# Maxima matmuls of two heads side by side on the two halves of the array, with a second copy of the odd heads' q and k

## The chip, the cores and the metric

One core of one Trainium2 chip runs the whole kernel. The metric is the device time of that core in microseconds (us), the median of three runs. The engines are TensorE (PE for its matmuls, PEld for its weight loads in the profile), VectorE (DVE), ScalarE (ACT), GpSimd (POOL) and SyncE (SP), which here only issues DMAs.

## The reference

A post-norm transformer block on x of 8 batches x 256 tokens x 128 features, in two layers.

```
q, k, v = x @ Wq.T + bq, x @ Wk.T + bk, x @ Wv.T + bv     # 16 heads of 64
q, k    = rope(q), rope(k)
attn    = softmax(q @ k.T / 8) @ v                        # per batch and head, 256 x 256
x       = layernorm(x + attn @ Wo.T + bo)
gates   = softmax(x @ gate_w); the best 2 of 8 experts, both weighted by the sum of their gates
x       = layernorm(x + sum over chosen experts of gelu(x @ w1[e] + b1[e]) @ w2[e] + b2[e], weighted)
```

The softmax needs the maximum of each row of q @ k.T, and how these row maxima come about is what the change is about.

## The kernel before, in words

**Units and slots.** The attention is cut into 16 units (`UNITS`) of 8 heads (`UH`); two units make a batch. Every engine runs the same hand-written order of slots T = -3 to 16, and slots 1 to 12 are three rounds of a hardware loop. In slot T the unit T is attended (scores, exp, times v), the row maxima of unit T + 1 are finished and those of unit T + 2 begun, and unit T + 3 is projected and rotated. Each slot has eight places i = 0 to 7. `maxima_at` gives the head whose maxima are found at place i: heads 3 to 7 of unit T + 1 at places 0 to 4, heads 0 to 2 of unit T + 2 at places 5 to 7. TensorE and VectorE walk these places in the same order, each in its own queue.

**Maxima.** For each head, `maxima` (line 348) issues two matmuls of 64 rows x 128 columns of weights and 256 moving columns: q of 128 tokens against k of all 256, contraction over the 64 features on partitions 0 to 63 of `qk`. Their results fill one PSUM bank, `ps_s[h % 2]`. VectorE's `row_maxima` (line 808) reduces the bank to two maxima per partition and raises `max_done`. The wait in `maxima` asks for the reduction of head h - 2, the last reader of that bank. At h == 0 `maxima` also waits for `qk_in`, that is, until all DMAs that bring unit u into `qk` have landed.

**From maxima to scores.** After head 7, `turn_maxima` (line 358) transposes the 16 columns of maxima, `read_mT` (line 815) copies them out, and a DMA of SP (line 299) writes them into row 64 of the q part of `qk`, whose k part holds ones there. So the matmuls of `scores` (line 365), which contract over all 128 partitions, subtract the maximum by themselves. ACT's exp reads `ps_t` (line 656), and `times_v` (line 375) multiplies by v in four matmuls of 65 columns per head.

**From projection to qk.** `project` (line 334) makes q and k of unit T + 3, ACT adds the bias (`raw`, line 638), VectorE multiplies by cosine and sine (line 785) and combines them in `rope` (lines 805 and 806), once for each half of the heads. The second `rope` stands at place 6, behind `find_maxima(5)`, which is the first head of unit T + 2, `read_mT`, `invert_sums`, `times_sin` and `find_maxima(6)`, and in every second slot behind `ln_one` step 1 (line 852) as well. When `rope_ready` has come, SP issues 8 DMAs of 64 KB (line 309) that gather the heads from `roped` into `qk`, one after another. The gate of unit u + 1 is then the wait at its head 0, at place 5 of the next slot.

**The rest.** In even slots from 2 on (`close`), the batch just finished is transposed (`turn_o`, line 395), multiplied by Wo (`out_proj`, line 405) and normalised by VectorE in ten small steps (`ln_one`, lines 852 to 892), most of them at places 6 and 7. `value` (line 345) makes v of a later unit at place 6 and waits for `ln_one` step 1 in those slots. The experts follow after slot 16 and are not touched.

Of the kernel before, what the change touches and what calls it, by code (L numbers as in the profile page):

```python
# [8 lines left out]
BF16 = mybir.dt.bfloat16  # L9
# [4 lines left out]
P = 128  # L14
S = 256
HID = 128
NH = 16
DH = 64
NB = 8
TOK = NB * S  # L20
UH = 8
# [9 lines left out]
EPS = 1e-5  # L31
EARLY = 3
M_ROW = 64
ROPE_DMAS = 8
TWO_ONES = 0x3F803F80


# [19 lines left out]
def postln_block(nc, x, packed_b, packed_f, expert_of, out):  # L57
# [15 lines left out]
    with ExitStack() as ctx:  # L73
        def sb(name, shape, dt):
            return ctx.enter_context(nc.sbuf_tensor(name, shape, dt))

        def sem(name):
            return ctx.enter_context(nc.semaphore(name))
# [29 lines left out]
        by_sin = sb("by_sin", [P, 2, 2, 2, S], BF16)  # L108
        roped = sb("roped", [P, 2, 2, 2, 2, S], BF16)
        qk = sb("qk", [P, 4, 2, UH, S], BF16)  # L110
        v_sb = sb("v_sb", [P, 2, 2, NH, DH + 1], BF16)
        row_max = sb("row_max", [P, 2, UH, QT], BF16)
        mT_sb = sb("mT_sb", [UH * QT, 2, P], BF16)
# [59 lines left out]
        def bank(name):  # L173
            return ctx.enter_context(nc.psum_tensor(name, [P, 512], F32))

        ps_s = [bank(f"ps_s{i}") for i in range(2)]
# [23 lines left out]
        qk_in = [sem(f"qk_in{i}") for i in range(4)]  # L200
# [3 lines left out]
        s_ready = sem("s_ready")  # L204
        max_done = sem("max_done")
# [50 lines left out]
        def need(eng, s, value):  # L256

            if isinstance(value, int) and value <= 0:
                return
            eng.wait_ge(s, value)  # L260

        def run(eng, slot):

            for T in range(-3, 1):
                slot(T, 0)
            with eng.Fori(0, 3) as it:
                for T in range(1, 5):
                    slot(T, it)
            for T in range(13, 17):
                slot(T, 0)  # L270

        def n(it, per_unit, units, more=0):

            return it * (4 * per_unit) + (per_unit * units + more)

        def has(T):

            return dict(attend=0 <= T < UNITS, maxima=0 <= T + 1 < UNITS, value=0 <= T + 2 < UNITS,
                        project=0 <= T + 3 < UNITS, close=T in range(2, UNITS, 2))


        @block.sync
        def _(sp):
            first, end = PACK_B["wqk0"][0], PACK_B["xT0"][1]
            sp.dma_start(in_b[:, first:end], packed_b[:, first:end]).then_inc(in_first, 16)
            sp.dma_start(in_b[:, 0:first], packed_b[:, 0:first]).then_inc(in_second, 16)
            sp.dma_start(in_b[:, end:COLS_B], packed_b[:, end:COLS_B]).then_inc(in_rest, 16)
            sp.dma_start(x_sb[:], x).then_inc(in_rest, 16)

            def slot(T, it):  # L290
                s = has(T)
                if s["maxima"]:
                    u = T + 1

                    need(sp, mT_ready, n(it, 1, u, 1))
                    if T == -1:
                        sp.wait_ge(pad_ready, 4)
                    dst = qk[M_ROW:M_ROW + 1, u % 4, 0, :, :]
                    sp.dma_start(dst, mT_sb[:, u % 2, :]).then_inc(m_in[u % 2], 16)
                if s["project"]:  # L300
                    u = T + 3

                    need(sp, rope_ready, n(it, 2, u, 2))
                    for g in range(4):
                        for half in range(2):
                            from_g = roped[32 * g:32 * g + 32, u % 2, half].rearrange("p a j s -> p (a j) s")
                            to = qk[32 * half:32 * half + 32, u % 4, :, :, :].rearrange(
                                "p a (j g) s -> p (a j) g s", g=4)[:, :, g, :]
                            sp.dma_start(to, from_g).then_inc(qk_in[u % 4], 16)
                if T == -3:  # L310
                    sp.dma_start(in_f[:], packed_f).then_inc(in_late, 16)
                    sp.dma_start(exp_of[:], expert_of).then_inc(in_late, 16)

            run(sp, slot)
            for p, (first, count) in enumerate(PIECES):
                sp.wait_ge(y_out, p + 1)
                sp.dma_start(out[:, first:first + count, :], y_sb[:, p % 2, 0:count]).then_inc(stored[p % 2], 16)
            for i in range(2):
                sp.wait_ge(stored[i], 16 * len(PIECES[i::2]))
# [3 lines left out]
        def _(pe):  # L323
# [22 lines left out]
                                 start=True, stop=True).then_inc(v_proj, 1)  # L346

            def maxima(u, h, it):
                if h == 0:
                    need(pe, qk_in[u % 4], it * (16 * ROPE_DMAS) + 16 * ROPE_DMAS * (u // 4 + 1))  # L350
                need(pe, max_done, n(it, UH, u, h - 1))
                for t in range(QT):
                    mm = nc.tensor.matmul(ps_s[h % 2][:, t * S:t * S + S],  # L353
                                          qk[0:DH, u % 4, 0, h, t * P:t * P + P],
                                          qk[0:DH, u % 4, 1, h, :], start=True, stop=True)
                mm.then_inc(s_ready, 1)

            def turn_maxima(u, it):
                take(1, mT_ready, n(it, 1, u, 1))
# [132 lines left out]
            def slot(T, it):  # L492
# [3 lines left out]
                def find_scores(i):  # L496
                    for u, h in maxima_at(T, i):
                        maxima(u, h, it)
# [269 lines left out]
        def _(dve):  # L768
# [27 lines left out]
            def rope(u, g, it):  # L796
# [3 lines left out]
                if g == 0:  # L800

                    w = 16 * ROPE_DMAS * ((u - 2) // 4 + 1)
                    need(dve, qk_in[(u - 2) % 4], it * (16 * ROPE_DMAS) + w)
                r, c, s = roped[:, u % 2, :, :, g, :], by_cos[:, g], by_sin[:, g]
# [433 lines left out]
```

## Time and profile before

| What | Value |
|---|---|
| Time, median of 3 runs | 293.36 us (292.1 to 294.01) |
| Profiled execution: its own time, its span | 295.25 us, 293.5 us |
| PE busy | 246.1 us (84%) |
| DVE busy | 235.9 us (80%) |
| ACT busy | 168.0 us (57%) |
| Mean granted clock of TensorE | 0.819 |

Busy times are those of the profiled execution. Ends of matmuls are modelled, so the starts of matmuls are the firmer marks. The granted clock is a share of 2.4 GHz; 0.50 is 1.2 GHz.

### The profile page before, as it was taken

The page shows a single profiled execution, that of the slowest core. Times are in us where ns is not written, and L with a number is a line of the kernel's source. Part 1 is how long each engine was busy: PE and PEld are TensorE (multiplying, and loading weights), DVE is VectorE, ACT ScalarE, POOL GpSimd, SP SyncE. Part 2 cuts the span into 40 slices and gives each one's busy share as a digit, 9 for nine tenths or more (in the row PEclk, how much of TensorE's full clock was granted, in tenths as well). Part 3 has the DMA queues.
Part 4 walks back from the last instruction along what each step waited for, and adds up shares of the span by engine and source line. Part 5 has one row for each costly group of instructions (what it writes and reads, how often), then busy time and mean ns, then how long its engine had stood idle before and what let it go on. Part 6 is the DMA issues. An engine that isn't in the chain of part 4 may idle for free.

```text
span 293.5 us, 5981 instructions
## 1 busy us (share of the span) xinstructions
PE 246.1 (84%) x1785; PEld 139.2 (47%) x1785; DVE 235.9 (80%) x688; ACT 168.0 (57%) x327; POOL 20.6 (7%) x34
## 2 busy tenths in 40 slices
PE   2737999997789789979988797999799938899991
PEld 0111345464446444645555355546545725466671
DVE  5898786969996989699798969897985794656985
ACT  3901556676858575846677574858534645545210
POOL 5000000000000000000000000000080010000121
PEclk9999999999955965685597859558855797999997
DMA  7153113030302021111113030303120000000012
GB/s 276 59 135 72 37 36 75 1 74 2 74 22 54 22 53 29 43 36 36 45 27 72 1 72 1 72 1 72 27 47 1 0 4 0 2 0 2 36 40 71
DMA packets 20438, 12.66 MB, mean 43 GB/s; under 512 B 2732, under 2 KB 19396, under 8 KB 20420
## 3 DMA queue, kind: packets, MB, share of 16 engines
q1 hardware_dynamic: 20420, 12.44, 16.5%
q8 instruction: 9, 0.15, 0.2%
q14 instruction: 9, 0.07, 0.1%
HBM read 2.92 MB, written 1.05 MB: 14 GB/s over the span
## 4 chain that ended last, share of the span: by engine, by line
issue 71%; PE 17%; DVE 7%; ACT 2%; POOL 2%; POOLq 0%; DVEq 0%
PE ps_o L487 4%; PE ps_s L461 3%; PE ps_t L370 2%; PE ps_s L353 2%; POOL sd L742 1%; PE ps_t L471 1%; PE ps_o L385 1%; PE ps_o L485 1%; ACT hg L715 1%; PE ps_m L448 1%; DVE qk L778 1%; DVE qk L777 1%; ACT oT_sb L651 1%; POOL rs L764 1%; PE ps_m L395 1%
## 5 line engine op out<-in xcount | busy, mean ns | idle before, releaser
L812 DVE TENSOR_REDUCE row_max<-ps_s 128x2 bf16<-128x512 f32 x128 | 86.7, 679 | 20.9 <-PE ps_s L353 19.7
L656 ACT ACTIVATE probs<-ps_t 128x512 bf16<-128x512 f32 x128 | 74.6, 606 | 35.4 <-PE ps_t L370 35.0
L353 PE MATMUL ps_s<-qk 64*128 64x256 bf16 x256 | 67.5, 359 | 7.5 <-DMA qk<-roped 4.8
L370 PE MATMUL ps_t<-qk 128*128 128x256 bf16 x256 | 66.5, 355 | 3.5 <-DMA qk<-mT_sb 1.7
L638 ACT ACTIVATE raw<-ps_m,bqk 128x256 bf16<-128x256 f32 x128 | 51.2, 478 | 9.3 <-PE ps_m L338 5.4
L385 PE MATMUL ps_o<-v_sb,probs 128*128 128x65 bf16 x512 | 46.5, 224 | 3.7 <-DVE o_sb L834 3.2
L385 PEld LDWEIGHTS ps_o<-v_sb,probs 128*128 128x128 bf16 x512 | 41.0, 121 | 16.2 <-issue 5.9
L645 ACT CAST v_sb<-ps_m 128x512 bf16<-128x512 f32 x32 | 17.5, 590 | 47.1 <-PE ps_m L345 47.1
L338 PE MATMUL ps_m<-in_b 128*128 (+1 forms) x128 | 35.3, 396 | 7.8 <-DMA in_b<-in_packed_b 4.6
L370 PEld LDWEIGHTS ps_t<-qk 128*128 128x128 bf16 x256 | 16.5, 106 | 42.3 <-issue 26.1
L834 DVE TENSOR_TENSOR o_sb<-ps_o,r_sum 128x256 bf16<-128x256 f32 x64 | 26.4, 412 | 0.1
L353 PEld LDWEIGHTS ps_s<-qk 64*128 64x128 bf16 x256 | 15.8, 103 | 22.5 <-DVE row_max L812 6.8
L338 PEld LDWEIGHTS ps_m<-in_b 128*128 128x128 bf16 x128 | 15.9, 135 | 19.0 <-ACT raw L638 7.8
L345 PE MATMUL ps_m<-in_b 128*128 128x512 bf16 x32 | 14.4, 525 | 12.3 <-DVE attn L852 9.1
L785 DVE TENSOR_TENSOR by_cos<-raw,in_b 128x1024 bf16<-128x1024 bf16 x32 | 21.9, 684 | 1.7 <-ACT raw L638 1.6
L742 POOL TENSOR_TENSOR sd<-ve,half_b 128x2 bf16<-128x2 bf16 x8 | 5.6, 705 | 239.9 <-DVE ve L879 239.9
L785 DVE TENSOR_TENSOR by_sin<-raw,in_b 128x1024 bf16<-128x1024 bf16 x32 | 21.4, 669 | 0.0
L715 ACT ACTIVATE hg<-ps_s,in_f 128x512 f32<-128x512 f32 x16 | 11.1, 691 | 17.1 <-PE ps_s L461 17.1
L825 DVE RECIPROCAL r_sum<-ps_o 128x4 f32<-128x4 f32 x64 | 11.1, 173 | 11.3 <-PE ps_o L385 10.7
L1104 DVE TENSOR_TENSOR hs<-hg,ps_t 128x512 f32<-128x512 f32 x16 | 11.0, 685 | 8.5 <-ACT hg L715 7.0
L651 ACT COPY oT_sb<-ps_m 128x1024 bf16<-128x1024 bf16 x16 | 15.7, 1036 | 1.0 <-PE ps_m L395 1.0
L487 PE MATMUL ps_o<-in_f,hs 128*128 128x128 f32 x112 | 16.2, 288 | 0.0
(105 smaller groups left out, 222.7 us busy)
## 6 DMA issues: line engine op xcount, KB each, us to landing
qk<-roped SPq DMA_DIRECT2D x128, 64.0 KB, 2.1
out<-y_sb SPq DMA_DIRECT2D x3, 256.0 KB, 2.1
in_b<-in_packed_b SPq DMA_DIRECT2D x1, 706.0 KB, 5.9
in_f<-in_packed_f SPq DMA_DIRECT2D x1, 586.0 KB
in_b<-in_packed_b SPq DMA_DIRECT2D x1, 516.0 KB, 3.8
in_b<-in_packed_b SPq DMA_DIRECT2D x1, 512.0 KB, 4.7
x_sb<-in_x SPq DMA_DIRECT2D x1, 512.0 KB, 6.7
qk<-mT_sb SPq DMA_DIRECT2D x16, 4.0 KB, 1.7
```

The costliest lines, as they stand in the source:

```text
L338: mm = nc.tensor.matmul(ps_m[a][:, half * S:half * S + S], wqk[u % 2][:, a, 2 * g + half, :], xT_sb[:, bass.ds(tok, S)], start=True, stop= ...
L353: mm = nc.tensor.matmul(ps_s[h % 2][:, t * S:t * S + S], qk[0:DH, u % 4, 0, h, t * P:t * P + P], qk[0:DH, u % 4, 1, h, :], start=True, sto ...
L370: mm = nc.tensor.matmul(ps_t[h % 2][:, c * S:c * S + S], qk[:, u % 4, 1, h, c * P:c * P + P], qk[:, u % 4, 0, h, :], start=True, stop=True)
L385: mm = nc.tensor.matmul(ps_o[(h // 2) % 2][:, col:col + DH + 1], probs[:, h % 4, c, t * P:t * P + P], v_sb[:, (u // 2) % 2, c, head, :], s ...
L487: mm = nc.tensor.matmul(y, hs[:, tc % 2, c, t * P:t * P + P], w2_sb[:, c, :], start=False, stop=(c == NE - 1))
L638: last = nc.scalar.activation(raw[:, u % 2, g, a, half, :], ps_m[a][:, half * S:half * S + S], ACT.Identity, bias=bqk[:, a, chunk:chunk + 1])
L645: nc.scalar.copy(v_sb[:, (u // 2) % 2, u % 2, UH * c:UH * c + UH, 0:DH], ps_m[c][:].rearrange("p (h d) -> p h d", d=DH)).then_inc(v_ready, 1)
L651: nc.scalar.copy(oT_sb[:, t].rearrange("p c s -> p (c s)"), ps_m[t][:].bitcast(BF16)).then_inc(oT_ready, 1)
L656: nc.scalar.activation(probs[:, h % 4].rearrange("p c s -> p (c s)"), ps_t[h % 2][:], ACT.Exp, scale=DH ** -0.5).then_inc(exp_done, 1)
L785: nc.vector.tensor_tensor(by[:, g].rearrange("p a h s -> p (a h) s"), raw[:, u % 2, g].rearrange("p a h s -> p (a h) s"), table[:].unsquee ...
L812: nc.vector.tensor_reduce(row_max[:, u % 2, h, :], ps_s[h % 2][:].rearrange("p (t s) -> p t s", s=S), AX_X, ALU.max, negate=True).then_inc ...
L834: nc.vector.tensor_tensor(o_sb[:, b % 2, :, head:head + 2, :].rearrange("p t h d -> p h t d"), o[:, :, 0:DH].rearrange("p (h t) d -> p h t ...
```

## The change

SP issues four more DMAs per unit: the odd groups of heads also go from `roped` to a new tensor `qk_odd`, on partitions 64 to 127, double buffered by unit. They raise the same semaphore as the eight others, so the gate of a unit now asks for twelve. `maxima` does nothing for an odd head. For an even head h it waits for the reductions up to head h - 1, and then issues the four matmuls of heads h and h + 1 in turn: even head from partitions 0 to 63 into `ps_s[0]`, odd head from partitions 64 to 127 into `ps_s[1]`. VectorE's work and order stay as they are.

```diff
-ROPE_DMAS = 8
+ROPE_DMAS = 12
...
+        qk_odd = sb("qk_odd", [P, 2, 2, UH // 2, S], BF16)
...
+                    for i in range(2):
+                        g = 2 * i + 1
+                        for half in range(2):
+                            from_g = roped[32 * g:32 * g + 32, u % 2, half].rearrange("p a j s -> p (a j) s")
+                            to = qk_odd[DH + 32 * half:DH + 32 * half + 32, u % 2, :, :, :].rearrange(
+                                "p a (j i) s -> p (a j) i s", i=2)[:, :, i, :]
+                            sp.dma_start(to, from_g).then_inc(qk_in[u % 4], 16)
...
             def maxima(u, h, it):
+
+                if h % 2 == 1:
+                    return
                 if h == 0:
                     need(pe, qk_in[u % 4], it * (16 * ROPE_DMAS) + 16 * ROPE_DMAS * (u // 4 + 1))
-                need(pe, max_done, n(it, UH, u, h - 1))
+                need(pe, max_done, n(it, UH, u, h))
                 for t in range(QT):
-                    mm = nc.tensor.matmul(ps_s[h % 2][:, t * S:t * S + S],
-                                          qk[0:DH, u % 4, 0, h, t * P:t * P + P],
-                                          qk[0:DH, u % 4, 1, h, :], start=True, stop=True)
-                mm.then_inc(s_ready, 1)
+                    even = nc.tensor.matmul(ps_s[0][:, t * S:t * S + S],
+                                            qk[0:DH, u % 4, 0, h, t * P:t * P + P],
+                                            qk[0:DH, u % 4, 1, h, :], start=True, stop=True)
+                    odd = nc.tensor.matmul(ps_s[1][:, t * S:t * S + S],
+                                           qk_odd[DH:P, u % 2, 0, h // 2, t * P:t * P + P],
+                                           qk_odd[DH:P, u % 2, 1, h // 2, :], start=True, stop=True)
+                even.then_inc(s_ready, 1)
+                odd.then_inc(s_ready, 1)
```

## Rows read from the trace of the kernel before

**Rows 1.** Page, part 1: busy time, share of the span, instructions.

```profile
PE 246.1 (84%) x1785; PEld 139.2 (47%) x1785; DVE 235.9 (80%) x688; ACT 168.0 (57%) x327; POOL 20.6 (7%) x34
```

**Rows 2.** Windows, TensorE alone: length, busy (count), granted clock, DMA share, GB/s.

```profile
40.00:43.00 3.00, 3.00 (x16) 1.00 0.00 0
...
85.00:88.00 3.00, 3.00 (x20) 0.50 0.22 50
...
100.00:103.00 3.00, 2.76 (x29) 1.00 0.29 66
```

**Rows 3.** Windows, one two-slot round: PE, PEld, DVE, ACT, POOL busy, clock, DMA.

```profile
109.17:123.45 14.28, 14.28 (x94) 8.09 (x92) 11.10 (x27) 10.10 (x20) 0.00 (x0) 0.54 0.16 37
123.45:137.62 14.17, 12.29 (x94) 7.06 (x91) 12.74 (x40) 8.81 (x20) 0.70 (x1) 0.70 0.16 37
```

**Rows 4.** Timeline at 1.2 GHz: start, length, engine, line, count, idle before.

```profile
107.87 0.60 PE L353 MATMUL ps_s<-qk 64*128 64x256 bf16 x2
108.41 0.13 PEld L370 LDWEIGHTS ps_t<-qk 128*128 128x128 bf16 x2 [0.41 <-issue]
...
108.81 0.43 PE L385 MATMUL ps_o<-v_sb,probs 128*128 128x65 bf16 x4
...
109.12 0.66 DVE L812 TENSOR_REDUCE row_max<-ps_s 128x2 bf16<-128x512 f32 x1
109.17 0.60 PE L353 MATMUL ps_s<-qk 64*128 64x256 bf16 x2
```

**Rows 5.** Timeline, TensorE, two and four matmuls of a projection at 1.2 GHz.

```profile
86.45 0.63 PE L338 MATMUL ps_m<-in_b 128*128 x2
...
88.18 1.06 PE L338 MATMUL ps_m<-in_b 128*128 x4
```

**Rows 6.** Timeline at 2.4 GHz, gate of unit 8 and the scores behind it.

```profile
123.45 0.39 PE L353 MATMUL ps_s<-qk 64*128 64x256 bf16 x2
...
123.77 0.39 PE L370 MATMUL ps_t<-qk 128*128 128x256 bf16 x2
```

**Rows 7.** Timeline at the start: DMAs of units 0 and 1, and their gates.

```profile
11.82 5.25 SPq L309 DMA_DIRECT2D qk<-roped  x8
...
18.56 0.61 PE L353 MATMUL ps_s<-qk 64*128 64x256 bf16 x2 [4.14 <-DMA qk<-roped]
...
21.09 5.10 SPq L309 DMA_DIRECT2D qk<-roped  x8
...
27.70 0.61 PE L353 MATMUL ps_s<-qk 64*128 64x256 bf16 x2 [0.63 <-DMA qk<-roped]
```

**Rows 8.** DMA issues by line: KB each, median us from issue to landing.

```profile
qk<-roped SPq DMA_DIRECT2D x128, 64.0 KB, 2.1
```

**Rows 9.** Timeline, from the gate of unit 7 (109.17) to unit 8's DMAs.

```profile
111.29 0.69 DVE L812 TENSOR_REDUCE row_max<-ps_s 128x2 bf16<-128x512 f32 x1
...
113.63 0.41 DVE L806 TENSOR_TENSOR roped<-by_cos,by_sin 128x512 bf16<-128x512 bf16 x1
...
114.06 5.13 SPq L309 DMA_DIRECT2D qk<-roped  x8
```

**Rows 10.** Timeline, from the gate of unit 8 to unit 9's DMAs, a closing slot.

```profile
127.32 0.40 DVE L852 TENSOR_TENSOR attn<-ps_m,v_bias 128x256 bf16<-128x256 f32 x1
...
128.41 1.89 SPq L309 DMA_DIRECT2D qk<-roped  x3
```

**Rows 11.** Timeline, TensorE, gates of unit 2 and of unit 15 (14 gates in all).

```profile
40.02 0.61 PE L353 MATMUL ps_s<-qk 64*128 64x256 bf16 x2
...
218.64 0.61 PE L353 MATMUL ps_s<-qk 64*128 64x256 bf16 x2
```

**Rows 12.** Timeline after a closing slot: maxima of head 4, reduction of head 3.

```profile
102.22 0.39 PE L353 MATMUL ps_s<-qk 64*128 64x256 bf16 x2
...
104.32 0.69 DVE L812 TENSOR_REDUCE row_max<-ps_s 128x2 bf16<-128x512 f32 x1 [0.26 <-issue]
```

**Rows 13.** Timeline at the start: the reductions of unit 0 and what they wait for.

```profile
21.78 0.28 DVE L898 CAST o_bias<-ps_m 128x128 bf16<-128x128 f32 x1
...
23.72 3.47 DVE L812 TENSOR_REDUCE row_max<-ps_s 128x2 bf16<-128x512 f32 x5 [1.07 <-PE ps_s L353]
24.47 1.20 PE L353 MATMUL ps_s<-qk 64*128 64x256 bf16 x4 [0.36 <-DVE row_max L812]
```

**Rows 14.** Waits of DVE from 40.02 to 218.64: total, times, longest.

```profile
DVE row_max L812 <- PE ps_s L353: 12.5, 22, 1.2
DVE r_sum L825 <- PE ps_o L385: 7.7, 10, 0.9
```

## The prediction

> **What bounds the kernel now.** I read the busy table first. TensorE is busy 84%, VectorE 80% [rows 1], too close for shares to decide, so the next view is windows of 3 us along the attention. The reader is to see two regimes. Where the granted clock is 0.50 TensorE is busy 3.00 of 3.00 us; where it is 1.00 it has gaps [rows 2]. The windows before the first clock record show 1.00, but the maxima matmuls there last 0.61 us for two as at 0.50, not 0.39 as at 1.00 [rows 6, 11], so I count that stretch as 1.2 GHz. At the low level TensorE is the bound. Over a two-slot round of 28.45 us VectorE is busy 23.84 us, 12.74 in one half and 11.10 in the other [rows 3]; it is the next bound, and it still spends 12.5 us on waits for maxima and 7.7 us on waits for times v between 40 and 218.6 us [rows 14]. The measure of progress is the gate, the first maxima matmul of each unit: from unit 2 at 40.02 to unit 15 at 218.64, 13 slots in 178.62 us, 13.74 us each or 27.5 us per two [rows 11].
>
> **Less work on TensorE.** At 1.2 GHz the two matmuls of one head occupy TensorE from 107.87 to 108.41, 0.54 us [rows 4]. Two of 256 columns stream in 0.43 us, the difference between four and two in a row [rows 5]; the other 0.11 us lies ahead of the next weight load, which sat idle for 0.41 us on "issue" behind the maxima [rows 4]. At 2.4 GHz a head costs 0.32 us [rows 6]. A pair costs between 0.54 us (the halves run fully side by side) and 0.97 us (one after the other, 4 x 0.213 + 0.11). I take 0.64, as one weight load of about 0.1 us must come before the second half starts. A dropped odd head also drops the way back into 64-row matmuls: four of 65 columns stream in 0.22 us at 1.2 GHz, and the next maxima start 0.36 us after them [rows 4], so that way costs 0 to 0.14; I take 0.1. A pair saves 2 x 0.54 - 0.64 + 0.1 = 0.54 us at 1.2 GHz, four pairs about 2.2 us per slot.
>
> By the Trainium skill, TensorE: Matmul & The Clock Gate, Part 3 (The mechanism), matmuls on different row groups run concurrently and start about 4 ns apart. By it the pair would cost 0.54 and not 0.64 us, and with the sum below, where a pair stands once in each return leg, the result would be about 1.4 us lower. No run shown yet has such a pair.
>
> **Four more DMAs on SP's queue, on the path.** Eight issues take 5.25 us at the start and 5.13 in the steady state, 0.65 us each [rows 7, 9], and a DMA lands 2.1 us after its issue [rows 8]. The gate opens at the last landing: unit 0's first issue is at 11.82 and its gate at 18.56; unit 1's are 21.09 and 27.70. So the way from first issue to open gate is 6.7 us with eight [rows 7], and with twelve 6.7 + 4 x 0.65 = 9.3 us. Bounds: 6.7, if the new copies were issued in no time, and 10.1, if each also added half a transfer time; I keep 9.3, the rate of the rows being the same in two stages.
>
> Is that hidden? Before, unit 7's gate is at 109.17, unit 8's DMAs start at 114.06 and its gate is at 123.45, 9.4 us later [rows 6, 9]: 2.7 us of slack with eight, 0.1 with twelve. In other slots the distance is smaller, so the DMAs become the gate. Then a loop closes over each slot. Gate of unit u; return leg to the first DMA of unit u + 1; 9.3 us to its gate. The return leg is what VectorE does from place 5 to the second rope. Before it is 4.89 us (109.17 to 114.06) in one slot and 4.96 us (123.45 to 128.41) in the closing one, but VectorE came to the head only at 111.29 [rows 6, 9, 10]. If it stands waiting at the gate, it starts 0.64 us after it, needs 111.29 to 114.06 = 2.77 us of work, and waits some 0.65 us for times v of head 3, which TensorE reaches behind the pair, scores and transpose: 4.1 us. In a closing slot step 1 of the normalisation adds 0.4 us [rows 10] and some 0.1 of wait, 4.6 us, up to 5.0 where the output projection runs at 1.2 GHz. Two slots: 4.1 + 4.6 + 2 x 9.3 = 27.3 us, up to 27.7. What is queued behind the gate on TensorE is everything: scores, transpose, times v and so exp and VectorE's next inputs. SP itself has room: its twelve issues end 7.8 us after the first, and the next mT DMA comes later than that.
>
> **The stricter wait.** Head h now waits for the reduction of h - 1. After a closing slot the maxima of head 4 were issued at 102.22 and the reduction of head 3, behind the LayerNorm steps, ended at 104.32 + 0.69 = 105.01 [rows 12]: 2.8 us late. At head 0 of unit 7 it would be 0.6 us (109.17 against 109.12 + 0.66) [rows 4]. VectorE is the late one there and loses only what TensorE needs to restart, about 0.64 us less the 0.4 us of other work that stands between, plus what times v comes later: 0.3 to 1.5 us per closing slot. VectorE's bound for two slots is then 23.84 plus waits; with 1.8 us of waits per slot as before (23 us of 13 slots with the small ones) [rows 14], 27.4 us. So chain and VectorE stand at the same length, and I take 27.5 us per two slots, no gain against 27.5. TensorE's 2.2 us per slot go into its waiting at the gate.
>
> **The start.** Unit 0's gate moves by 2.6 us to 21.2. VectorE then reduces head 0 and reads the biases, ending near 23.6 (before, 21.78 + 0.28) [rows 13], and head 1 by 24.3. Before, the reductions ran back to back at 0.69 us, with TensorE filling one bank while the other was read [rows 13]. Now each pair is 2 x 0.69 us of reductions and then about 0.75 us of restart: head 6 ends near 29.9, two products of 0.65 follow, head 7 ends at 31.9. Unit 1's DMAs would have landed at 21.09 + 9.3 = 30.4, but its pair waits for head 7: gate at 32.0 in place of 27.70. Unit 2's first DMA comes at about 36.0, and its gate at 45.3 in place of 40.02: +5.3 us. Slots 2 and 3, without LayerNorm, take 13.4 us each, as before.
>
> **The end.** From unit 15's gate on there are no rope DMAs. Four pairs at 1.2 GHz remain: -2.2 us. What follows is unchanged.
>
> **Sum.** Against the profiled execution's 295.25 us (span 293.5 and 1.75 around it): +5.3 at the start, 0 in 13 slots, -2.2 at the end, +3.1. I take half a microsecond off for the first slots' pairs at 1.2 GHz, where a little less TensorE work precedes each rope: +2.6. The median of the runs shown is 293.36, so 296 us, 0.9% slower. The profiled run lies 0.6% above the median; the difference is carried over, not the level.
>
> **Rivals.**
> - **TensorE's relief wins.** If copies land sooner than I add (6.7 to 8 us to the gate), the return leg no longer closes the loop and VectorE bounds: 23.84 us and about 2 of waits, 25.9 per two slots. From unit 4 on that is 5.5 x (27.6 - 25.9) = -9.4; with +4.3 at the start and -2.2 at the end, about 286 us. For it: TensorE was saturated at the low clock [rows 2]. Against: the serial issue on SP [rows 7, 9]. A middle case, waits of 1.4 us a slot, gives 291. The Trainium skill's TensorEngine Tiling (Array Packing), PSUM Bottleneck, says that tiling does not speed up the emptying of PSUM, which may then bound; VectorE's 23.84 of 28.45 us agrees, and it is this case's floor.
> - **The halves don't run side by side.** The pair costs 0.97, 0.33 more than I took, once in each return leg and 14 times: +4.6, and the tail saves 1.1 less: 302 us. For it: matmuls on TensorE start in the order of the queue, and no row before shows two at once.
> - **The stricter wait decides (the other side).** The place is head 4 behind a closing slot, the price 1.3 us of VectorE each, decisive as soon as VectorE comes to head 3 later than TensorE comes to head 4, which 102.22 against 105.01 shows. Six such slots give +7.8 us on top of the start: about 303 us if VectorE and not the DMA loop sets the round.
> - **The clock.** More waiting at gates may keep the clock at 0.50 for longer; the return legs of six closing slots rise by 0.4: +2.4, 298 us. It lies inside the forecast's range.
>
> **Chances and range.** Forecast 0.55 (291.5 to 300), TensorE's relief 0.2 (half of it at 286, half at 291), serial halves 0.1, stricter wait 0.15. A change of 1% is about what a measurement of this kernel can tell: 290.4 and 296.3 bound "same". From the forecast 0.02 faster, 0.27 same, 0.26 slower; relief gives 0.14 faster and 0.06 same; the other two are slower but for 0.03. So faster 0.16, same 0.36, slower 0.48. The range 288 to 303 leaves out half of the relief case and a little of the others.
>
> **What would show it.** In the profile after: twelve issues in about 7.8 us per unit; TensorE's idle time ahead of the maxima put down to the DMA of `roped`, about ten times; 9.3 us from first issue to gate; gates 13.7 us apart; unit 2's gate near 45; a pair that ends within 0.65 to 0.75 us. I am wrong if the gates wait for nothing, if the first two gates move by less than 2 us, or if the gaps at maxima are those behind VectorE's reductions.

## The result, and the profile after

The changed kernel takes 305.6 us (median of 4 runs, 304.14 to 307.35) against 293.69 us before (292.1 to 294.05); the ratio is 1.042, 95% interval 1.034 to 1.050. I had forecast 296 us with a range up to 303: the sign was right, the size three to five times too small. The profiled execution is the shortest run, 304.14 us with a span of 302.3, and that of the kernel before, 295.25 us with a span of 293.5, lies above its other four; so the traces show 8.8 us of the 11.9 us between the medians, and the rest is the scatter of the runs. Medians and ranges are of all runs; the ratios, here and below, leave out runs that lie more than 1.5% above the fastest of their kernel.

First the busy line of the page (busy time, share of the span, instructions), to be held against [rows 1].

```profile
PE 203.5 (67%) x1785; PEld 122.0 (40%) x1785; DVE 238.0 (79%) x688; ACT 166.4 (55%) x327; POOL 20.6 (7%) x34
```

TensorE lost 43 us of busy time and the kernel became longer, so in the changed kernel TensorE's work no longer sets the pace. Next the view of waits of the changed kernel (total, times, longest).

```profile
PE ps_s L364 <- DVE row_max L827: 34.0, 26, 3.2
...
PE ps_s L364 <- DMA qk_odd<-roped: 30.5, 10, 6.7
...
DVE row_max L827 <- PE ps_s L367: 27.0, 42, 2.0
```

Two new waits stand ahead of the maxima matmuls (line 364), of nearly the same size: one for the last copy into `qk_odd` (30.5 us), one for VectorE's reductions (34.0 us). VectorE in its turn waits 27.0 us for the maxima. These are two of the mechanisms of the prediction, at once; the first is the sign that it had named for the forecast, about ten waits for the DMA, the second one that it had named against it.

The timeline shows where each acts: the gates of units 8, 9 and 10 with the rope DMAs between them, answering [rows 4, 6, 9].

```profile
131.91 0.39 PE L364 MATMUL ps_s<-qk 64*128 64x256 bf16 x1 [2.61 <-DMA qk_odd<-roped]
131.91 0.39 PE L367 MATMUL ps_s<-qk_odd 64*128 64x256 bf16 x1
...
132.45 0.61 PE L385 MATMUL ps_t<-qk 128*128 128x256 bf16 x2
...
136.41 5.21 SPq L310 DMA_DIRECT2D qk<-roped  x8
141.66 2.53 SPq L317 DMA_DIRECT2D qk_odd<-roped  x4
...
147.20 0.28 PE L364 MATMUL ps_s<-qk 64*128 64x256 bf16 x1 [1.45 <-DVE row_max L827]
...
151.43 5.11 SPq L310 DMA_DIRECT2D qk<-roped  x8
156.58 2.53 SPq L317 DMA_DIRECT2D qk_odd<-roped  x4
...
160.56 0.28 PE L364 MATMUL ps_s<-qk 64*128 64x256 bf16 x1 [2.84 <-DMA qk_odd<-roped]
```

From 151.43 to 160.56 are 9.13 us from first issue to gate, near the forecast 9.3; the gate opens with the DMA. But between 136.41 and 147.20 are 10.8 us: there the last DMA had landed at 145.65, and the gate waited for the reduction of head 7. The reader is to see two kinds of slots, closing ones (with the LayerNorm) and plain ones. The windows say the same (columns as in [rows 3]).

```profile
131.91:147.20 15.29, 10.31 (x91) 6.48 (x92) 12.00 (x36) 8.45 (x18) 0.69 (x1) 0.79 0.23 52
147.20:160.56 13.36, 7.47 (x91) 4.93 (x91) 12.10 (x29) 10.15 (x20) 0.00 (x0) 1.00 0.26 59
```

The closing slot takes 15.29 us and is set by VectorE: 12.00 us of work, and 3.29 us in which it is idle, 2.7 of them waiting for TensorE (0.7 in the closing slot of [rows 3]). The plain one takes 13.36 us and is set by the DMA loop. Together 28.65 us, against the 27.5 that I had taken. Inside the closing slot the loss begins behind the LayerNorm. The timeline of the changed kernel there:

```profile
136.49 0.28 PE L364 MATMUL ps_s<-qk 64*128 64x256 bf16 x1
...
139.97 0.42 DVE L907 TENSOR_SCALAR x<-attn,rs 128x128 bf16 x2
140.31 0.68 DVE L827 TENSOR_REDUCE row_max<-ps_s 128x2 bf16<-128x512 f32 x1
...
141.05 0.28 PE L364 MATMUL ps_s<-qk 64*128 64x256 bf16 x1 [2.42 <-DVE row_max L827]
...
141.47 0.69 DVE L827 TENSOR_REDUCE row_max<-ps_s 128x2 bf16<-128x512 f32 x1 [0.15 <-PE ps_s L367]
...
142.62 0.18 DVE L840 RECIPROCAL r_sum<-ps_o 128x4 f32<-128x4 f32 x1 [0.46 <-PE ps_o L400]
...
144.58 0.69 DVE L827 TENSOR_REDUCE row_max<-ps_s 128x2 bf16<-128x512 f32 x1 [0.84 <-PE ps_s L367]
```

Heads 2 and 3 are issued at 136.49 and stand ready; head 3 is reduced at 140.31, after `ln_one`. TensorE stands still for 2.42 us until then, starts heads 4 and 5 at 141.05, and everything that it does from there on is late: VectorE waits 0.15 us for head 4, 0.46 us for times v, 0.84 us for head 6. The 2.42 us of TensorE would be nothing, VectorE being busy; the 1.45 us of VectorE are the price.

Over the whole, the gates of units 2 and 15, against [rows 11], and what the stretches between them took:

```profile
45.73 0.39 PE L364 MATMUL ps_s<-qk 64*128 64x256 bf16 x1 [3.51 <-DMA qk_odd<-roped]
...
231.03 0.28 PE L364 MATMUL ps_s<-qk 64*128 64x256 bf16 x1 [0.31 <-DMA qk_odd<-roped]
```

| Stretch | Before | After | Difference | Forecast |
|---|---|---|---|---|
| to the gate of unit 2 | 40.02 | 45.73 | +5.7 | +5.3 |
| 13 slots, to the gate of unit 15 | 178.62 | 185.30 | +6.7 | 0 (and -0.5 for the first slots) |
| to the end of the span | 74.9 | 71.3 | -3.6 | -2.2 |

The 6.7 us lie in the closing slots alone. The six of them (from the gates of units 4, 6, 8, 10, 12 and 14 to the next) took 82.1 us before and 91.3 us after, 9.3 more; the seven plain ones took 96.6 and 94.0 us, 2.6 less.

### The profile page after: what moved, and what is told of

Same layout as the page of the kernel before. It is cut to its first block, busy times and chain, and to the rows that moved or that the text cites. A ratio compares the mean times of both kernels' runs of the same rounds, so it can differ in the third digit from the quotient of the medians.

```text
span 302.3 us, 6036 instructions
## 1 busy us (share of the span) xinstructions
PE 203.5 (67%) x1785; PEld 122.0 (40%) x1785; DVE 238.0 (79%) x688; ACT 166.4 (55%) x327; POOL 20.6 (7%) x34
## 4 chain that ended last, share of the span: by engine, by line
issue 73%; PE 14%; DVE 7%; ACT 2%; POOL 2%; DMA 1%; POOLq 0%; DVEq 0%
PE ps_o L502 4%; PE ps_s L476 3%; POOL sd L757 1%; PE ps_t L486 1%; DVE row_max L827 1%; PE ps_t L385 1%; ACT oT_sb L666 1%; PE ps_o L500 1%; DMA qk<-mT_sb 1%; ACT hg L730 1%; PE ps_m L420 1%; PE ps_m L463 1%; DVE qk L793 1%; DVE qk L792 1%; POOL rs L779 1%
## 5 line engine op out<-in xcount | busy, mean ns | idle before, releaser
L827 DVE TENSOR_REDUCE row_max<-ps_s 128x2 bf16<-128x512 f32 x128 | 86.8, 681 | 27.9 <-PE ps_s L367 27.0
L364 PE MATMUL ps_s<-qk 64*128 64x256 bf16 x128 | 32.2, 344 | 64.6 <-DVE row_max L827 34.0
L385 PE MATMUL ps_t<-qk 128*128 128x256 bf16 x256 | 61.4, 332 | 4.6 <-ACT probs L671 3.2
L653 ACT ACTIVATE raw<-ps_m,bqk 128x256 bf16<-128x256 f32 x128 | 50.4, 479 | 3.8 <-DVE bqk L795 3.8
L400 PE MATMUL ps_o<-v_sb,probs 128*128 128x65 bf16 x512 | 43.6, 216 | 4.2 <-DVE o_sb L849 3.8
L400 PEld LDWEIGHTS ps_o<-v_sb,probs 128*128 128x128 bf16 x512 | 37.5, 114 | 16.4 <-issue 7.9
L346 PE MATMUL ps_m<-in_b 128*128 (+1 forms) x128 | 29.8, 345 | 12.6 <-ACT raw L653 7.2
L364 PEld LDWEIGHTS ps_s<-qk 64*128 64x128 bf16 x128 | 7.7, 101 | 74.3 <-DVE row_max L827 37.1
L367 PE MATMUL ps_s<-qk_odd 64*128 64x256 bf16 x128 | 32.3, 344 | 0.0
L385 PEld LDWEIGHTS ps_t<-qk 128*128 128x128 bf16 x256 | 17.7, 107 | 24.7 <-issue 17.5
L346 PEld LDWEIGHTS ps_m<-in_b 128*128 128x128 bf16 x128 | 11.9, 114 | 25.2 <-ACT raw L653 16.5
```

What stands on the lines that cost most here:

```text
L346: mm = nc.tensor.matmul(ps_m[a][:, half * S:half * S + S], wqk[u % 2][:, a, 2 * g + half, :], xT_sb[:, bass.ds(tok, S)], start=True, stop= ...
L364: even = nc.tensor.matmul(ps_s[0][:, t * S:t * S + S], qk[0:DH, u % 4, 0, h, t * P:t * P + P], qk[0:DH, u % 4, 1, h, :], start=True, stop= ...
L367: odd = nc.tensor.matmul(ps_s[1][:, t * S:t * S + S], qk_odd[DH:P, u % 2, 0, h // 2, t * P:t * P + P], qk_odd[DH:P, u % 2, 1, h // 2, :], ...
L385: mm = nc.tensor.matmul(ps_t[h % 2][:, c * S:c * S + S], qk[:, u % 4, 1, h, c * P:c * P + P], qk[:, u % 4, 0, h, :], start=True, stop=True)
L400: mm = nc.tensor.matmul(ps_o[(h // 2) % 2][:, col:col + DH + 1], probs[:, h % 4, c, t * P:t * P + P], v_sb[:, (u // 2) % 2, c, head, :], s ...
L653: last = nc.scalar.activation(raw[:, u % 2, g, a, half, :], ps_m[a][:, half * S:half * S + S], ACT.Identity, bias=bqk[:, a, chunk:chunk + 1])
```

## The experiments

All ratios are to the kernel before, run beside each.

**Copies and gate alone.** `maxima` as before, with the change's twelve DMAs and its gate of twelve.

> The four extra DMAs per unit and the gate of twelve, but the maxima matmuls and their wait as before. Theory 1 (each slot is set by its own longest: the DMA gate in plain slots, the reductions in closing slots; the two add): the way from first issue to gate is 9.3 us, unit 2's gate moves by about 5 us, and the slots that took 12.3 to 13.1 us take 13.5 to 14, so 300 to 304 us. Theory 2 (the copies alone make the whole loss): 304 to 307 us. Theory 3 (only the stricter wait costs): within 2 us of before.

Measured: 303.74 us, ratio 1.040 (1.034 to 1.045). Its view of waits has the DMA ahead of the maxima twelve times:

```profile
PE ps_s L361 <- DMA qk_odd<-roped: 26.8, 12, 6.7
```

So the copies on the path cost 4% where nothing is paired. The time lies at the upper end of theory 1 and just below theory 2; it speaks against theory 3.

**The stricter wait alone.** The kernel before with one line changed:

```diff
-                need(pe, max_done, n(it, UH, u, h - 1))
+                need(pe, max_done, n(it, UH, u, h - h % 2))
```

> The kernel before with one edit: an even head waits for the reduction of the head just before it, the odd head waits as before. No copies, no pairs. Theory 1: TensorE stalls at heads 0, 4 and 6 behind VectorE, 1 us or more per slot, so 298 to 304 us. Theory 2: within 2 us of before. Theory 3: 304 to 307 us.

Measured: 310.8 us, ratio 1.058 (1.047 to 1.069). All three theories are off: the wait alone costs more than the whole change, and theory 1's 298 to 304 was too low. Both costs are real, and each alone, on a TensorE without the pairs' relief, loses as much as the whole change (4.2%) or more. Their sum, 9.8%, is more than twice the change's 4.2%, so the pairs give back a good part, or the costs cover each other. The next experiments remove them one at a time from the changed kernel.

**Fine gates.** The same twelve DMAs in another order on three semaphores; heads 0, 1, 4, 5 need the first four, 2, 3, 6, 7 the next, `scores` the last.

```diff
+                    for g, odd, done in ((0, 0, qk_in), (1, 1, qk_in), (2, 0, qk_in2), (3, 1, qk_in2),
+                                         (1, 0, qk_in3), (3, 0, qk_in3)):
...
+                if h == 2:
+                    need(pe, qk_in2[u % 4], it * 64 + 64 * (u // 4 + 1))
```

> The changed kernel with its twelve DMAs in another order and on three semaphores: heads 0, 1, 4 and 5 wait for four DMAs (about 4.1 us from the first issue), heads 2, 3, 6 and 7 for the next four, the scores for the last four. Theory 1: no gate waits for a DMA any more except at the start, the closing slots stay at 15.3 us and the plain ones fall to 12 to 13, so 295 to 300 us, 5 to 10 below the changed kernel. Theory 2: back at 293 or below. Theory 3: no change from 305.6.

Measured: 290.29 us, ratio 0.992 (0.988 to 0.997). The gate of twelve cost 5 points of ratio. It was the gate and its order, not the traffic: all twelve DMAs are still issued on the same queue. The number is the one that theory 2 gave, 293 or below, and under theory 1's 295 to 300; but the slots are theory 1's. The plain ones fell, to 11.6 to 12.2 us and so further than its 12 to 13, and the closing ones stayed long, as it has it (gates 30.3, 41.9, 54.0, 65.6, then 80.9 and 92.5: steps of 11.6, 12.1, 11.6, then 15.3 and 11.6).

**Reductions of a pair together.** At the place of the even head VectorE reduces both.

```diff
                     for u, h in maxima_at(T, i):
-                        row_maxima(u, h, it)
+                        if h % 2 == 0:
+                            row_maxima(u, h, it)
+                            row_maxima(u, h + 1, it)
```

> The changed kernel, but VectorE reduces both heads of a pair at the place of the even head, so that the banks are free one place earlier. Twelve DMAs and gate as in the change. Theory 1: closing slots fall from 15.3 to the DMA loop's 13.6 to 14, plain slots stay at 13.4, so about 296 to 300 us. Theory 2: no change from 305.6. Theory 3: back at 293 or below.

Measured: 299.97 us, ratio 1.027 (1.021 to 1.034), as theory 1 has it. The DMA now stands ahead of the maxima 15 times with 41.6 us, and at every gate but that of unit 1, so the loop took over the closing slots too.

**Both.**

> The gates of the fine-gates kernel and the reductions of a pair at one place together. Theory 1 (the DMA gate and the stricter wait are the two costs, and they add because each slot is set by its own longest): with both gone VectorE's work is the bound, 23.8 us and some 2 of waits per two slots, so 280 to 286 us. A rival: the pairs' own gain is small and what is left is VectorE and the clock, so no better than the fine gates alone, 288 to 291 us.

Measured: 291.86 us, ratio 0.994 (0.990 to 0.998). Here theory 1 failed, and the time came out just above the rival's 288 to 291. The waits of TensorE for reductions fell from the 42.1 us of the fine-gates kernel to 12.8, but its wait for the copy of the maxima grew from 6.3 us in 8 to this:

```profile
PE ps_m L357 <- DVE mT_sb L842: 24.5, 9, 3.1
```

By the order of the code, with heads 0 and 1 reduced together, `read_mT` stands behind one more reduction, and `value`, which needs its PSUM bank, waits for `read_mT`, with all of TensorE behind it. My repair had its own stall.

**The pair on one half.** The changed kernel, the odd head reading `qk` on partitions 0 to 63 as the even one does.

> The changed kernel with twelve DMAs, the gate and the stricter wait, but the odd head's two matmuls read q and k from partitions 0 to 63 of qk like the even head's, so a pair streams one after the other. If the side-by-side halves save 0.43 us per pair at 1.2 GHz and 0.21 at 2.4, and that lies on the path at the gates and restarts: 308 to 316 us. If the halves' overlap is off the path: 304 to 307 us, as the change.

Measured: 313.15 us, ratio 1.067 (1.061 to 1.074), 2.5 points or 7.5 us above the change. The overlap of the halves lies on the path even there.

**The kernel before with two gates**, its eight DMAs on two semaphores.

> The kernel before, its eight DMAs unchanged, but the gate of heads 0, 1, 4, 5 asks for the first four and that of heads 2, 3, 6, 7 for the others. It tells what finer gates give without pairs. In the kernel before the gates wait only for units 0 and 1, so 1 to 4 us less at the start: 289 to 293 us. If it equals the fine-gates kernel (290.3), the pairs there gave nothing.

Measured: 291.33 us, ratio 0.991 (0.987 to 0.995). Unit 0's gate is 2.6 us earlier, unit 1's 0.4 (27.3), and unit 2's stays at 40.0. Its time equals that of the fine-gates kernel, but its slots do not: the fine-gates kernel takes 9.2 us less in the seven plain slots (84.0 against 93.2) and 10.0 more in the six closing ones (91.8 against 81.9). So there the pairs' gain was just eaten by the stricter wait.

**Both repairs on one half.** Pairs from `qk` alone, eight DMAs with two gates, pairs reduced together.

> Pairs issued together but both from partitions 0 to 63, no copies, eight DMAs with two gates, reductions of a pair together. It is the kernel with both costs removed less the side-by-side halves and the copies. Theory 1: TensorE's work is that of before less a quarter of the switches, so 284 to 292 us, and the difference to the kernel with both fixes, 3 to 8 us, is what the two halves are worth. Rival: the halves are worth nothing in time because VectorE bounds, and the two are within 2 us.

Measured: 300.94 us, ratio 1.017 (1.008 to 1.026). The time is well above the 284 to 292 expected; the mT wait of that repair (20.7 us in 8) is in both kernels. Above the kernel with both repairs and the two halves it is 9 us by medians and 2.3 points, some 7 us, by the ratios; the second is inside the 3 to 8 expected.

**Heads 0 and 1 at their own places again**, the other pairs reduced together.

> Fine gates, and the reductions of heads 2 and 3, 4 and 5, 6 and 7 together, but those of heads 0 and 1 at their own places, so that read_mT and value are not behind one more reduction. If the kernel with both fixes lost to that new wait (24.5 us in 9 waits of value for the copy of the maxima), this one is at 283 to 288 us. If VectorE bounds in any order, it stays at 289 to 292 us.

Measured: 289.58 us, ratio 0.979 (0.974 to 0.984). It is 1.5 points better than with heads 0 and 1 together, and cannot be told to belong to one case: the median lies in the second, 289 to 292, while a ratio of 0.979 would be 288 us, at the end of the first. It does not tell what the mT wait was worth, because the wait did not go:

```profile
PE ps_m L357 <- DVE mT_sb L842: 17.3, 8, 2.2
```

Why it stayed at 17.3 us was not tried.

**Only heads 2 and 3 together.** Head 3 comes at place 7, ahead of the LayerNorm steps, all else at its own place.

```diff
                     for u, h in maxima_at(T, i):
-                        row_maxima(u, h, it)
+                        if h not in (3,):
+                            row_maxima(u, h, it)
+                        if h in (2,):
+                            row_maxima(u, h + 1, it)
```

> Fine gates, and only the reductions of heads 2 and 3 together: the reduction of head 3 no longer stands behind the LayerNorm steps of the closing slot. If that place is the price of the stricter wait (closing slots of 15.3 to 16.1 us against 14.1 before), closing slots fall below 14.5 us and the time to 284 to 288 us. If the wait costs at every pair, at most 2 us below the fine gates alone, 288 to 291 us.

Measured: 280.4 us (279.2 to 282.22), ratio 0.953 (0.949 to 0.958), faster than expected and the fastest of all kernels here, 4.7% below the kernel before. One reduction moved by one place is worth 3.9 points against the fine gates alone. In the traces the closing slots are 9.1 us shorter together, the plain ones 2.2; the mT wait is down to 2.1 us in 3. The six runs also had a higher granted clock, 0.878 to 0.920 against 0.836 to 0.871 with the fine gates alone; how much of the gain is the clock's was not separated. The windows of a closing and a plain slot, as above:

```profile
116.72:130.68 13.96, 8.75 (x92) 5.22 (x93) 12.87 (x40) 9.33 (x20) 0.70 (x1) 0.87 0.30 69
130.68:142.19 11.51, 8.62 (x92) 5.28 (x93) 10.70 (x26) 8.95 (x19) 0.00 (x0) 0.86 0.24 55
```

Two slots take 25.47 us, and VectorE is busy in 23.57 of them: it is the nearest bound, as the prediction's first rival said it would be, close to the 25.9 us it named. TensorE still waits for reductions in this kernel, and longer than in the changed one:

```profile
PE ps_s L370 <- DVE row_max L835: 36.8, 38, 2.7
```

These waits cost little here, because VectorE is itself busy in all but 1.9 us of the two slots.

**The single gate with heads 2 and 3 together.**

> The changed kernel with its twelve DMAs and single gate, and only the reductions of heads 2 and 3 together. With the wait behind the LayerNorm gone, the DMA loop sets every slot at 13.4 to 13.9 us: 14 gates, about 1.5 us less in each of six closing slots, so 295 to 298 us. If the stricter wait elsewhere also holds the gates, 300 us or more.

Measured: 296.9 us, ratio 1.012 (1.004 to 1.020), inside the first case. From unit 2 on the steps between its gates are 13.1 to 14.3 us throughout, 13.6 on average; the wait for the DMA is there twelve times:

```profile
PE ps_s L364 <- DMA qk_odd<-roped: 36.3, 12, 6.7
```

**The 280.4 us kernel on one half**, with eight DMAs and two gates.

> The 280.4 us kernel (fine gates, heads 2 and 3 reduced together) without side-by-side halves: a pair's four matmuls all read qk on partitions 0 to 63, there are eight DMAs and two gates, and no copies. If the two halves are what makes that kernel fast: 286 to 291 us. If VectorE bounds and TensorE's saving is hidden: 279 to 283 us, and the copies were never needed.

Measured: 292.39 us, ratio 0.994 (0.989 to 0.999), 4.1 points or 12 us slower than with the halves (8.2 us between the two traces), just above the 286 to 291 expected. VectorE's work is the same, 152.3 us against 151.6 between the gates of units 2 and 15; it waits longer for the maxima, 18.2 us against 12.9 over the span. A pair there and in the changed kernel, from its first matmul to the scores behind it, at 1.2 GHz; first this kernel's timeline:

```profile
109.18 0.39 PE L359 MATMUL ps_s<-qk 64*128 64x256 bf16 x1 [1.66 <-DVE row_max L823]
109.37 0.42 PE L362 MATMUL ps_s<-qk 64*128 64x256 bf16 x1
109.58 0.42 PE L359 MATMUL ps_s<-qk 64*128 64x256 bf16 x1
109.80 0.42 PE L362 MATMUL ps_s<-qk 64*128 64x256 bf16 x1
110.15 0.61 PE L380 MATMUL ps_t<-qk 128*128 128x256 bf16 x2
```

The four matmuls start one after the other, 0.97 us for the pair. On two halves those of heads 0 and 1 start together, and it is 132.45 - 131.91 = 0.54 us, as for a single head before [rows 4].

The two repairs on the changed kernel, as ratios to before:

| | reductions at their places | heads 2 and 3 together |
|---|---|---|
| gate of twelve | 1.042 | 1.012 |
| fine gates | 0.992 | 0.953 |

The fine gates are worth 5.0 to 5.9 points and the moved reduction 3.0 to 3.9, whether or not the other is there. Where they act is told by the gates in the traces, one profiled execution of each kernel, in us:

| Kernel | to the gate of unit 2 | six closing slots | seven plain slots | behind the gate of unit 15 |
|---|---|---|---|---|
| before | 40.0 | 82.1 | 96.6 | 74.9 |
| before, stricter wait alone | 42.3 | 94.1 | 96.0 | 76.1 |
| before, copies and gate alone | 43.4 | 85.0 | 97.9 | 74.1 |
| changed | 45.7 | 91.3 | 94.0 | 71.3 |
| changed, heads 2 and 3 together | 45.3 | 84.1 | 93.2 | 71.9 |
| fine gates | 41.9 | 91.8 | 84.0 | 71.8 |
| fine gates, heads 2 and 3 together | 42.2 | 82.7 | 81.8 | 73.5 |

The fine gates take 10.0 and 11.5 us from the plain slots and 3 to 4 us from the start, and next to nothing from the closing ones; the moved reduction takes 7.2 and 9.1 us from the closing slots and 0.7 and 2.2 from the plain ones. The stricter wait alone adds 12.0 us to the closing slots and nothing to the plain ones. That is what settles the cause: two costs that add, because they sit in different slots.

## Why the prediction was right or wrong

- **What bounds the kernel; less work on TensorE.** Right. Relief on TensorE is real once it may work: the halves are worth 12 us in the 280.4 us kernel. Of my bounds for a pair, 0.54 and 0.97 us, both were measured, 0.54 with the halves and 0.97 without; the 0.64 that I took, for a weight load, was too much. Here the rule of the Trainium skill, TensorE: Matmul & The Clock Gate, Part 3 (The mechanism), that matmuls on different row groups start about 4 ns apart, was better than my reading. The trace agrees: the two starts are at 131.91 both, and over all 64 pairs they lie 3 to 6 ns apart.
- **Four more DMAs on the path.** Right in mechanism and size: 9.13 us from first issue to gate against 9.3 (from first issue to last landing 9.1 to 9.8 for 14 of the 16 units, 10.2 and 10.7 for the other two); return legs of 4.5 us (131.91 to 136.41) and 4.2 us (147.20 to 151.43) against 4.6 and 4.1. With the stricter wait's place repaired, the kernel with the single gate runs at 13.6 us per slot and 296.9 us, near the 13.7 and 296 of the forecast.
- **The stricter wait: the step that failed.** I wrote that "chain and VectorE stand at the same length, and I take 27.5 us per two slots". I had added up each bound over two slots, 27.3 and 27.4, and taken the larger. But each slot is set by its own longest: the closing slot by VectorE (15.29 us), the plain one by the DMA loop (13.36 us). The two-slot length is the sum of the maxima, 28.65 us here, and not the maximum of the sums. That is only part of it: my own terms, slot by slot, are 13.4 us of loop against 11.10 + 1.8 = 12.9 of VectorE, and 13.9 against 12.74 + 1.8 = 14.5, and the larger ones add up to 27.9. The rest is a term that I had priced and then put at nothing: 0.3 to 1.5 us per closing slot for the stricter wait, while I took 1.8 us of waits in every slot "as before". VectorE was idle for 3.29 us in the closing slot shown. With this term added, my own numbers give 28.2 to 29.4 us, and the measured 28.65 lies in between. Over the 13 slots it is 6.7 us, where I had put 0. The rival that named place and price (head 4 behind a closing slot, 1.3 us) was right in both, with 1.45 us of VectorE's waits in the trace; I had priced it as an alternative to the DMA loop and not as an addition. Its time, about 303 us, was the nearest of all that I wrote down.
- **The start.** Right: gates at 21.12, 31.72 and 45.73 against 21.2, 32.0 and 45.3. For the last of them two small errors met: unit 2's first DMA came at 35.45 and not at 36.0, and its twelve took 10.2 us to land and not 9.3.
- **The end.** Mis-sized: -3.6 us, not -2.2. Not taken apart further.
- **The halves don't run side by side.** Refuted: 0.54 against 0.97 us.
- **The clock.** As a rival I had more waiting keep the clock low. It did not: the mean granted clock of the profiled executions is 0.819 before and 0.848 after. Nor did it clearly rise, for the four runs of the changed kernel lie between 0.810 and 0.848, and those of the kernel before, run beside the experiments, between 0.773 and 0.853.

## What to carry to other kernels

Where two bounds stand at nearly the same length, work out the maximum of each slot and add these up, not the sums over a round: bounds that take turns add. Before two operations are issued together, ask what the second one's buffer did for the first: with both banks filled at once, the producer runs one step less ahead, and the consumer's longest detour (here the LayerNorm between two reductions) comes onto the path; moving one reduction ahead of the detour was worth 3.0 to 3.9 points here. And a transfer added to a group that is awaited as a whole delays all of its readers; give each reader its own semaphore, first needed first sent.

## What the runs showed of the hardware

- Matmuls of 64 rows on the two halves of the array, into two PSUM banks, start 3 to 6 ns apart and cost what one costs: 0.54 us per pair at 1.2 GHz, and at 2.4 GHz 147.53 - 147.20 = 0.33 us against 0.32 us for one head before [rows 6].
- The slots in which TensorE was less busy had the higher granted clock. Before, a slot in which it was busy 14.28 of 14.28 us had a mean of 0.54 [rows 3]; after, one with 7.47 of 13.36 us had 1.00, and the 280.4 us kernel has 0.897 over its span. Which of the two brings about the other is not shown: at 1.2 GHz the same matmuls also last longer (0.54 us for a head's maxima against 0.32), and so fill more of a slot.

```profile
core 0: 280.2 us, clock 0.897
```

What lifts it in the 280.4 us kernel was not tried by itself.
- Four more DMAs per unit, half as many again, are not waited for once the first matmuls do not ask for the last of them: in the fine-gates kernel TensorE waits for one of these DMAs once, for 1.5 us at the start, although twelve still take 9.1 us from first issue to last landing in most units. No run has the copies without pairs and without a wait, so a small cost of the traffic itself is not excluded.
